# Layer 1's transposed rows h2 kept in DRAM and read back by layer 2, in a four-layer graph network on one Trainium2 core

## The reference, cut to what matters

```
h0 = relu(layernorm(x));  x = x + L0(h0)          # weighted sums over edges, times a 256x256 matrix
h1 = relu(layernorm(x));  x = x + L1(h1)          # degree rows, edge sums, two sigmoid gates
h2 = relu(layernorm(x));  x = x + L2(h2)          # attention over edges, then a feed-forward net
h3 = relu(layernorm(x));  x = x + L3(h3)          # relation sums, then a GRU cell

def L2(h2):                                       # q, k, v = h2 @ wq + bq, h2 @ wk + bk, h2 @ wv + bv
    out = segment_sum(softmax-weighted v[src], dst)
    t = layer_norm(h2 + out + h2 @ ws + bs, g1, b1)
    ffn = gelu(t @ w_ff1 + b_ff1) @ w_ff2 + b_ff2
    return layer_norm(t + ffn, g2, b2)
```

## Time and profile before

| what | value |
|---|---|
| median of 3 runs | 5362.05 us (5357.85 to 5363.22) |
| the profiled execution's own time | 5354.62 us |
| its span, first to last instruction | 5352.8 us |
| busy: PE, DVE, ACT, POOL | 67%, 73%, 27%, 69% of the span |
| mean granted TensorE clock | 0.944 of full speed |
| `layers_0_and_1` | about 2290 to 2665 us of the span |
| `attention` | about 2665 to 3850 us |
| `layer_2` | about 3850 to 4174 us |

### The profile page before, as it was taken

How to read it: one execution, slowest core, us unless ns; L and a number is a source line. 1 busy time by engine, 2 the same in 40 slices (tenths; PEclk the granted TensorE clock), 3 DMA queues, 4 the chain that set the end, 5 groups by cost and what they waited for, 6 DMA issues and landing times. The chain is left out here.

```text
span 5352.8 us, 103419 instructions
## 1 busy us (share of the span) xinstructions
PE 3567.2 (67%) x16542; PEld 2660.1 (50%) x16543; DVE 3920.0 (73%) x14051; ACT 1438.1 (27%) x4733; POOL 3693.7 (69%) x4313
## 2 busy tenths in 40 slices
PE   0000013535777777777689999999899688888887
PEld 0000001214555555554478888888799345555554
DVE  9949944757777777745688888888677666666665
ACT  0000000000000000033377777777666111111111
POOL 1777777775777777767666666666467777777774
PEclk9999999999999999968899999999999798888888
DMA  3333335434555555633233333333222333333332
GB/s 92 100 95 99 95 98 98 143 95 127 159 159 159 159 159 158 148 92 94 87 97 94 94 95 95 94 94 94 84 59 65 109 115 109 105 105 105 106 106 78
DMA packets 455298, 577.76 MB, mean 108 GB/s; under 512 B 82394, under 2 KB 357968, under 8 KB 455137
## 3 DMA queue, kind: packets, MB, share of 16 engines
q0 software_dynamic: 150496, 395.04, 25.4%
q1 hardware_dynamic: 304705, 181.71, 12.9%
HBM read 491.28 MB, written 86.76 MB: 108 GB/s over the span
## 5 line engine op out<-in xcount | busy, mean ns | idle before, releaser
L1329 POOL DMA_INDIRECT a_row<-h_rows,a_idx x832 | 787.4, 946 | 370.5 <-PE a_p_s L1455 198.1
L444 POOL DMA_INDIRECT src_records<-rec,pos_slot x784 | 791.8, 1010 | 355.0 <-issue 243.3
L1945 POOL DMA_INDIRECT r_row<-h_rows,r_idx x832 | 806.6, 969 | 316.5 <-issue 162.1
L815 POOL DMA_INDIRECT s_row<-h_rows,s_rec x832 | 788.9, 948 | 294.3 <-issue 170.1
L827 PE MATMUL s_sums<-s_row,s_hotw 128*128 128x256 f32 x1664 | 575.2, 428 | 387.0 <-DVE s_hotw L850 198.0
L1986 PE MATMUL r_p_s<-r_row,r_hot 128*128 128x272 f32 x1664 | 634.9, 499 | 213.9 <-DVE r_row L2120 206.0
L1986 PEld LDWEIGHTS r_p_s<-r_row,r_hot 128*128 128x128 f32 x1664 | 358.4, 234 | 501.7 <-DVE r_row L2120 221.8
L1432 PE MATMUL a_p_q<-nodes,a_hotT 128*128 x1664 | 570.3, 425 | 55.5 <-DVE a_score L1499 55.1
L857 DVE TENSOR_TENSOR nodes<-nodes,s_sums 128x385 f32 x832 | 460.9, 554 | 151.1 <-PE s_sums L828 137.9
L827 PEld LDWEIGHTS s_sums<-s_row,s_hotw 128*128 128x128 f32 x1664 | 252.6, 191 | 528.9 <-issue 263.3
L1455 PE MATMUL a_p_s<-a_row,a_masked 128*128 128x257 f32 x1664 | 497.0, 380 | 2.0 <-DVE sums L1536 1.3
(11 more groups left out here) (310 smaller groups left out, 8196.9 us busy)
## 6 DMA issues: line engine op xcount, KB each, us to landing
s_rec<-src_records SPq DMA_DIRECT2D x832, 66.0 KB, 2.0
rec<-in_edge_attr SPq DMA_DIRECT2D x98, 448.0 KB
s_row<-h_rows,s_rec POOLq DMA_INDIRECT x832, 2.7
a_row<-h_rows,a_idx POOLq DMA_INDIRECT x832, 2.8
r_row<-h_rows,r_idx POOLq DMA_INDIRECT x832, 2.8
src_records<-rec,pos_slot POOLq DMA_INDIRECT x784
h_rows<-H SPq DMA_DIRECT2D x1, 6272.0 KB, 27.7
x_rows<-nodes SPq DMA_DIRECT2D x49, 128.0 KB, 1.9
```

The source lines that it names most:

```text
L444: gp.indirect_dma_start(out=src_records, out_offset=bass.IndirectOffsetOnAxis(ap=pos_slot[:, k:k + 1], axis=0), in_=rec[:, k, :], in_offse ...
L815: gp.indirect_dma_start(out=row[:, k, :], out_offset=None, in_=env["h0_rows"], in_offset=bass.IndirectOffsetOnAxis(ap=rec[:, k, DST:DST + ...
L1329: gp.indirect_dma_start(out=row[:, k, 0:D], out_offset=None, in_=env["h2_rows"], in_offset=bass.IndirectOffsetOnAxis(ap=idx[:, k:k + 1], a ...
L1945: gp.indirect_dma_start(out=row[:, k % R, 0:D], out_offset=None, in_=env["h3_rows"], in_offset=bass.IndirectOffsetOnAxis(ap=idx[:, k:k + 1 ...
```

## The change

In layer 1 the buffer `turned_h` gets six slots instead of two, and SyncE stores each transposed block to a new DRAM table `h2_turned` (lag `AHEAD` + 11 = 15). ScalarE's copy waits for the product of six blocks earlier and for the store of six blocks earlier, where it waited for the product of two blocks earlier. In layer 2 SyncE loads the transposed block beside the plain one into `hin_t`; `turn_rows` transposes the attention sums alone, `copy_rows` copies 256 columns instead of 512, and `project` waits for the loaded block and takes it as the left factor for ws. The plain h2 rows are still stored and loaded, since the attention gathers and `add_bs` use them.

```diff
--- before.py
+++ after.py
@@ -216,6 +216,7 @@
                    src_records=src_records, by_dst=by_dst, table_rows=table_rows)
         env["x_rows"] = dram("x_rows", (NODES_PAD, D))
         env["h2_rows"] = dram("h2_rows", (NODES_PAD, D))
+        env["h2_turned"] = dram("h2_turned", (NODES_PAD, D))
         env["h3_rows"] = dram("h3_rows", (NODES_PAD, D))
         prepare(env)
         with ExitStack() as mid:
@@ -923,7 +924,7 @@
         added = sb(ctx, "added_terms", [P, TB, D])
         h1 = sb(ctx, "h1", [P, 2, D])
         h2 = sb(ctx, "h2", [P, TB, D])
-        turned_h = sb(ctx, "turned_h", [P, 2, DC, P])
+        turned_h = sb(ctx, "turned_h", [P, TB, DC, P])
         half = sb(ctx, "n_half", [P, 1])
 
         st, mv, rstd, nmr = (sb(ctx, "n_" + n, [P, 2, TB, w]) for n, w in (("st", 6), ("mv", 2), ("rstd", 1), ("nmr", 1)))
@@ -945,6 +946,7 @@
         z_in = [sem(f"z_in{k}") for k in range(TB)]
         x2_stored = [sem(f"x2_stored{k}") for k in range(TB)]
         h2_stored = [sem(f"h2_stored{k}") for k in range(TB)]
+        h2t_stored = [sem(f"h2t_stored{k}") for k in range(TB)]
         LOADS = 12
 
         def row(name):
@@ -1008,11 +1010,18 @@
                     own_wait(sp, S["h2_ready"], i + 1)
                     sp.dma_start(rows_view(env["h2_rows"], i), h2[:, k:k + 1, :]).then_inc(h2_stored[k], 16)
 
+                def store_turned_h2(i, k, opening, g):
+                    own_wait(sp, S["h2_copied"], i + 1)
+                    sp.dma_start(rows_view(env["h2_turned"], i),
+                                 turned_h[:, k, :, :].rearrange("p j n -> p (j n)").rearrange("p (a d) -> p a d", a=1)
+                                 ).then_inc(h2t_stored[k], 16)
+
                 in_turns(sp, BLOCKS, TB, (GATE_ARGS + 1, load_vectors), (0, load_x), (AHEAD + X2, store_x2),
-                         (AHEAD + H2, store_h2), peeled=PEELED)
+                         (AHEAD + H2, store_h2), (AHEAD + COPY_H, store_turned_h2), peeled=PEELED)
                 for k in range(TB):
                     sp.wait_ge(x2_stored[k], 16 * ROUNDS[k])
                     sp.wait_ge(h2_stored[k], 16 * ROUNDS[k])
+                    sp.wait_ge(h2t_stored[k], 16 * ROUNDS[k])
 
             @block.gpsimd
             def _(gp):
@@ -1114,7 +1123,7 @@
                     if not opening or k >= 1:
                         pe.wait_ge(S["q_ready"], i)
                     for j in range(DC):
-                        last = nc.tensor.matmul(p_q, turned_h[:, k % 2, j, :], qk[:, j, :],
+                        last = nc.tensor.matmul(p_q, turned_h[:, k, j, :], qk[:, j, :],
                                                 start=j == 0, stop=j == DC - 1)
                     last.then_inc(S["h2_qk"], 1)
 
@@ -1167,9 +1176,10 @@
 
                 def copy_h2(i, k, opening, g):
                     ac.wait_ge(S["h2_turned"], i + 1)
-                    if not opening or k >= 2:
-                        ac.wait_ge(S["h2_qk"], i - 1)
-                    nc.scalar.activation(turned_h[:, k % 2, :, :], p_th, ACT.Copy).then_inc(S["h2_copied"], 1)
+                    if not opening:
+                        ac.wait_ge(S["h2_qk"], i - TB + 1)
+                        ac.wait_ge(h2t_stored[k], g * 16)
+                    nc.scalar.activation(turned_h[:, k, :, :], p_th, ACT.Copy).then_inc(S["h2_copied"], 1)
 
 
                 in_turns(ac, BLOCKS, TB, (COPY_H, copy_h2), (COPY, copy_turned), (GATES, gates), (NORM1, norm_x1),
@@ -1561,9 +1571,10 @@
         b_ff1 = sb(ctx, "b_ff1_cols", [P, FC])
         vec = {n: sb(ctx, "e_" + n, [P, D]) for n in ("bv", "bs", "g1", "b1", "g2", "b2", "b_ff2")}
         hin = sb(ctx, "e_hin", [P, TB, D])
+        hin_t = sb(ctx, "e_hin_t", [P, TB, DC, P])
         xin = sb(ctx, "e_xin", [P, TB, D])
         staged = sb(ctx, "e_staged", [P, 2, D])
-        turned = sb(ctx, "e_turned", [P, 2, 2 * DC, P])
+        turned = sb(ctx, "e_turned", [P, 2, DC, P])
         biased = sb(ctx, "e_biased", [P, 2, D])
         norm1 = sb(ctx, "e_norm1", [P, 2, D])
         y = sb(ctx, "e_y", [P, 2, D])
@@ -1575,7 +1586,7 @@
         inv, coef = (sb(ctx, "e_" + n, [P, BLOCKS]) for n in ("inv", "coef"))
 
         st, mv, rstd, nmr = (sb(ctx, "e_" + n, [P, 3, TB, w]) for n, w in (("st", 6), ("mv", 2), ("rstd", 1), ("nmr", 1)))
-        p_t = ps(ctx, "e_p_t", [P, 2 * DC, P])
+        p_t = ps(ctx, "e_p_t", [P, DC, P])
         p_ty = ps(ctx, "e_p_ty", [P, DC, P])
         p_o = [ps(ctx, f"e_p_o{k}", [P, D]) for k in range(2)]
         p_f = [ps(ctx, f"e_p_f{k}", [P, FC, P]) for k in range(2)]
@@ -1589,6 +1600,7 @@
                                                       for n in ("stated", "averaged", "with_eps", "rooted", "scaled"))
         h2_in = [sem(f"e_h2_in{k}") for k in range(TB)]
         x2_in = [sem(f"e_x2_in{k}") for k in range(TB)]
+        h2t_in = [sem(f"e_h2t_in{k}") for k in range(TB)]
         h3_stored = [sem(f"e_h3_stored{k}") for k in range(TB)]
         LOADS = 5 + len(vec)
 
@@ -1619,6 +1631,12 @@
                         own_wait(sp, S["res1_done"], i - TB + 1)
                     sp.dma_start(hin[:, k:k + 1, :], rows_view(env["h2_rows"], i)).then_inc(h2_in[k], 16)
 
+                def load_turned_h2(i, k, opening, g):
+                    if not opening:
+                        own_wait(sp, S["projected"], i - TB + 1)
+                    sp.dma_start(hin_t[:, k, :, :].rearrange("p j n -> p (j n)").rearrange("p (a d) -> p a d", a=1),
+                                 rows_view(env["h2_turned"], i)).then_inc(h2t_in[k], 16)
+
                 def load_x2(i, k, opening, g):
                     if not opening:
                         own_wait(sp, S["x3_ready"], i - TB + 1)
@@ -1628,7 +1646,7 @@
                     own_wait(sp, S["h3_ready"], i + 1)
                     sp.dma_start(rows_view(env["h3_rows"], i), h3[:, k:k + 1, :]).then_inc(h3_stored[k], 16)
 
-                in_turns(sp, BLOCKS, TB, (0, load_h2), (RES2, load_x2), (AHEAD + H3 + 1, store_h3), peeled=PEELED)
+                in_turns(sp, BLOCKS, TB, (0, load_h2), (0, load_turned_h2), (RES2, load_x2), (AHEAD + H3 + 1, store_h3), peeled=PEELED)
                 for k in range(TB):
                     sp.wait_ge(h3_stored[k], 16 * ROUNDS[k])
 
@@ -1666,21 +1684,20 @@
 
                 def turn_rows(i, k, opening, g):
                     pe.wait_ge(S["staged"], i + 1)
-                    pe.wait_ge(h2_in[k], g * 16 + 16)
                     if not opening or k >= 1:
                         pe.wait_ge(S["copied"], i)
                     for j in range(DC):
-                        nc.tensor.transpose(p_t[:, j, :], staged[:, k % 2, j * P:(j + 1) * P], c["ident"][:])
-                        last = nc.tensor.transpose(p_t[:, DC + j, :], hin[:, k, j * P:(j + 1) * P], c["ident"][:])
+                        last = nc.tensor.transpose(p_t[:, j, :], staged[:, k % 2, j * P:(j + 1) * P], c["ident"][:])
                     last.then_inc(S["turned"], 1)
 
                 def project(i, k, opening, g):
                     pe.wait_ge(S["copied"], i + 1)
                     if not opening or k >= 2:
                         pe.wait_ge(S["res1"], i - 1)
-                    for n, w in enumerate((wv, ws)):
+                    pe.wait_ge(h2t_in[k], g * 16 + 16)
+                    for n, (t, w) in enumerate(((turned[:, k % 2], wv), (hin_t[:, k], ws))):
                         for j in range(DC):
-                            last = nc.tensor.matmul(p_o[k % 2], turned[:, k % 2, n * DC + j, :], w[:, j, :],
+                            last = nc.tensor.matmul(p_o[k % 2], t[:, j, :], w[:, j, :],
                                                     start=n + j == 0, stop=n + j == DC)
                     last.then_inc(S["projected"], 1)
```

## The result

| | before | changed |
|---|---|---|
| first comparison, median of 10 and 10 runs | 5359.54 us (5351.78 to 5364.24) | 5344.41 us (5338.18 to 5349.00) |
| its ratio | | 0.9972 (95%: 0.9962 to 0.9982), 15.0 us (9.6 to 20) |
| second comparison, median of 15 and 11 runs | 5358.15 us (5345.82 to 5362.87) | 5346.60 us (5336.64 to 5352.51) |
| its ratio | | 0.9979 (95%: 0.9970 to 0.9988), 11.3 us (6.4 to 16) |
| the profiled executions | 5354.62, span 5352.8 | 5344.43, span 5342.6 |

The account below looks back on a forecast made before the run. TensorE was taken to bound layer 2's steady part, POOL close behind and bounding layer 1. 10.7 us of transposes less 1.0 for POOL's last positions gave 9.7, so 5362.05 became 5352.3 us, range 5346.5 to 5359.5.

Parts of the forecast that it names:

- 98 transposes at 0.109 us, 10.7 us on TensorE: Layer 2: two transposes fewer per block, all on a TensorE without idle time; its position falls from 5.90 to 5.68 us.
- the 0.1 at half clock: Start of layer 2, first three blocks at half clock: at most 0.1 us more over the sum, left out.
- The copy, the waits, layer 1's store, the traffic: 0.: ScalarE's shorter copy hidden, waits, stores and DMA traffic free: 0 each, at worst 1 us for start or layer 1.
- It follows at 5.68: Layer 2: POOL (GpSimd) keeps TensorE's faster pace of 5.68 us, its need being elastic, set by alignment with VectorE's instructions.
- The 5.24 of the pair 3972.86 and 3978.10: Layer 2: two successive ends of POOL's position without a wait between, read as its need per position, 5.24 us.
- The 5.41: Layer 2: POOL's need in the earlier stretch, from 5.90 less 0.49 us of longer chains per position.
- I take 1.0 us off: End of layer 2's steady part: POOL's last four positions stay at 24.2 us against TensorE's 22.3, costing 1.0 us.
- Rival A: Layer 2: POOL stays ahead, its end chain starts some 1.5 us sooner; gain 12.2 us, time 5349.9; chance 0.24.
- B: Layer 2: POOL becomes the bound, nothing gained from 3981 on; gain 5.9 us, time 5356.2; chance 0.16.
- D: Layer 1: added stores lengthen POOL's gathers by 0.28 us each; 17 us slower, time 5379; chance 0.05.
- C: End of layer 2: something outside takes the gain back, so it is hidden altogether; time 5362; chance 0.05.
- The base: Whole kernel: the median time of 5362.05 us before the change, from which the predicted 9.7 us was taken.

## Why the prediction was off

The direction and the main mechanism were right, and the size was short.

- *98 transposes at 0.109 us, 10.7 us on TensorE.* Right. The step fell to 5.68 us, TensorE's stretch by 11.1 in the first pair of traces, by 10.7 between the two kernels that differ in the transposes alone. The 0.4 beyond is of the size of the 0.1 at half clock that I had left out, and of the scatter.
- *The copy, the waits, layer 1's store, the traffic: 0.* Right each: 282.1 with the wide copy; no wait of `project`; layer 1 within 0.8 us; the transfers at most 1.1 us at the start, about the 1 us that I kept for it.
- *"It follows at 5.68", an elastic need.* Right, and so is the reason that I gave, that the need is set by how GpSimd's instructions fall against VectorE's: 5.0 to 5.1 us of work, and 0.59 us of waiting for VectorE inside the records at 5.68 against 0.85 at 5.90. But I had no number for the room that is left, and 0.19 us more was already too much. The 5.24 of the pair 3972.86 and 3978.10 was one short position of an alternating 5.24 and 6.56, not a rate. The 5.41 fits the earlier stretch (5.90 less 4.3 us of waits in nine positions is 5.42), but it isn't the need at another alignment: where GpSimd waited for nobody it took 5.84 with the small addition.
- *"I take 1.0 us off" for GpSimd's last four positions.* This is the step that failed, and the term of the sum that was mis-sized: it was a gain of 1.4. I took 24.2 us for four positions as what GpSimd needs there ("POOL's side stays"), and TensorE's 22.3 as running away from it. It didn't stay: the four took 22.6. GpSimd was late in the kernel before because of the slip at 3981 (a phase of +0.3 instead of -0.5 to -1.2), and the two traces with the slip have a tail 1.1 to 1.5 us longer than the kernels without it and with the same chains. The changed kernel comes to the last block 0.18 us ahead, its tail is 14.4 instead of 15.8. Two kernels show that this isn't the pace: with transfers and transposes, and with the small addition in the kernel before, the pace is the old one, there is no slip, and the tails are 14.7 and 14.4. Why the slip follows the late instruction in the kernel before alone stays open; no experiment moved the alignment by itself.
- *Rival A* had the right size, 12.2 us, by this mechanism (a "lead over VectorE at the last block" larger by some 1.5 us, and a chain to the end that starts as much sooner), and a wrong sign to know it by: no waits of GpSimd for VectorE came back. It deserved more than 0.24. *B* is refuted by the pace of 5.68 and by the kernel before with one addition more, *D* by 1233 and 956 ns, *C* by the stage.
- *The base.* 5362.05 was a median of three; the two later medians of the same kernel are 5359.54 and 5358.15. Of the 7.9 us between 5352.3 and 5344.41, 2.5 are this, 2.8 the mis-sized term and the 0.4, and the rest is within the interval of the comparison; the second gave 5346.60.

The Trainium skill's rule of the lock ("SBUF — State Buffer", section "SBUF: two separate sides") with its full price kept would have given 5.9 us. The traces agree with the rule itself: GpSimd's long records overlap VectorE's instructions with two SBUF inputs and end a fixed time after them. They don't agree with the full price: it fell from 0.85 to 0.59 us per block. A GpSimd instruction that comes earlier only waits longer for the same end, so this part of its length is for the most part time that GpSimd had.

## What to carry to other kernels

Where one engine has no waits and still keeps exactly another's pace, its records can contain its slack, and their sum is no need. Compare each kind of record with its shortest, and look which instruction of the other engine runs beside the longer ones. Test the room: add a small instruction per turn, and see whether the pace holds. Here 0.19 us more per block was free before the change and cost 7 us after it. And in an engine that is the bound, a tiny dependent instruction costs its length and both gaps around it, 0.44 us for 0.23 busy, so moving one to an engine with room is worth more than its row says.

## What the runs showed of the hardware

- A 1-column addition on GpSimd was recorded as 191 ns, or as 367 to 376 when a VectorE instruction with two SBUF inputs ran beside it; the root (`e_rstd`) as 567 ns, or up to 869. VectorE's product was held up likewise, 0.68 us instead of 0.42 behind a 256-column addition of GpSimd.
- Whole chips differed: up to `source_sums` 1242 to 1254 us on some, 1647 to 1707 on others, `attention` 1185 against 1777 to 1838, with layers 1 and 2 equal to about a microsecond, although layer 1 issues two indirect gathers per block. The median of their issues was 1.16 and 0.96 us on both kinds.
- A GpSimd 0.16 us per block too slow cost TensorE nothing for some 30 blocks, and then 4.7 us in the last ones.
